# Expert stages: one row tile in four of the closing gated add goes from VectorE to GpSimd

## The reference, cut to what matters

```python
# block 2 (stage l0f): one expert per row
idx = jnp.argmax(logits, axis=-1)
gates = softmax(logits)[idx]
for ei in range(8):
    h = gelu(xf @ W1[ei] + b1[ei]); y = h @ W2[ei] + b2[ei]
    out = out + y * (gf * mask)[:, None]
x = x + out
# block 6 (stage l2f): two experts per row
topv, topi = jax.lax.top_k(logits, 2)
topw = softmax(topv)
out = sum over the two experts of topw * expert(xf)
x = x + out
```

## Time and profile before

| what | us |
|---|---|
| median of 3 runs | 2441.24 |
| the three runs | 2441.24, 2434.01, 2441.58 |
| time of the profiled execution | 2440.11 |
| its span in the profile | 2438.3 |
| VectorE busy in it | 1604.2 (66%) |
| TensorE busy in it | 1987.9 (82%) |
| GpSimd busy in it | 951.7 (39%) |

### The profile page before, as it was taken

How to read it: one execution, slowest core, us unless ns; L and a number is a source line. 1 busy time by engine, 2 the same in 40 slices (tenths; PEclk the granted TensorE clock), 3 DMA queues, 4 the chain that set the end, 5 groups by cost and what they waited for, 6 DMA issues and landing times. The chain is left out here.

```text
span 2438.3 us, 40723 instructions
## 1 busy us (share of the span) xinstructions
PE 1987.9 (82%) x13441; PEld 1621.2 (66%) x13441; DVE 1604.2 (66%) x5274; ACT 1183.1 (49%) x3293; POOL 951.7 (39%) x919
## 2 busy tenths in 40 slices
PE   8985999599948967976999947777878778777888
PEld 5663898499937855655999935566656666665555
DVE  6776111588974237854111168999999999995786
ACT  3544232455421115543333325687777787875444
POOL 3311454300007023303555425666666666662210
PEclk9997999655779989987999965577777678757899
DMA  3112565520315012315354330000000000101442
GB/s 97 62 47 84 205 240 177 150 37 1 108 48 182 0 65 74 101 36 184 130 205 161 106 123 25 1 31 18 31 18 31 31 1 31 49 1 63 164 157 77
DMA packets 101861, 204.50 MB, mean 84 GB/s; under 512 B 20158, under 2 KB 70550, under 8 KB 93718
## 3 DMA queue, kind: packets, MB, share of 16 engines
q1 hardware_dynamic: 77568, 116.19, 14.3%
q0 software_dynamic: 23808, 85.50, 10.2%
q10 hardware_dynamic: 280, 0.23, 0.0%
HBM read 216.24 MB, written 55.28 MB: 111 GB/s over the span
## 5 line engine op out<-in xcount | busy, mean ns | idle before, releaser
L833 DVE MATCH_REPLACE8 l3a_left<-l3a_top,l3a_left 128x256 f32<-128x256 f32 x768 | 308.3, 409 | 0.0
L826 DVE MAX8 l3a_top<-l3a_left 128x8 f32<-128x256 f32 x768 | 285.5, 413 | 0.0
L525 POOL TENSOR_TENSOR l3a_prob<-l3a_expd,l3a_rest 128x512 f32<-128x512 f32 x128 | 162.8, 1272 | 211.4 <-ACT l3a_rest L608 210.4
L363 PEld LDWEIGHTS l3a_psO<-l3a_probT,l3a_vp 128*128 128x128 f32 x1024 | 185.5, 269 | 69.7 <-ACT l3a_probT L624 40.6
L363 PE MATMUL l3a_psO<-l3a_probT,l3a_vp 128*128 128x128 f32 x1024 | 210.0, 370 | 24.7 <-ACT l3a_probT L624 24.6
L345 PE MATMUL l3a_psT<-all_ident,l3a_prob 128*128 128x128 f32 x512 | 112.8, 361 | 106.0 <-POOL l3a_prob L525 105.2
L512 POOL TENSOR_TENSOR l3a_kept<-l3a_raw_sc,l3a_mone 128x512 f32<-128x512 f32 x128 | 163.7, 1279 | 71.9 <-ACT l3a_raw_sc L592 67.9
L2043 ACT ACTIVATE l2f_hT<-l2f_psH,l2f_wt 128x128 f32<-128x128 f32 x312 | 89.2, 369 | 209.8 <-PE l2f_psH L1997 209.8
L518 POOL TENSOR_TENSOR l3a_sc_sb<-l3a_kept,l3a_mlow 128x512 f32<-128x512 f32 x128 | 164.1, 1282 | 10.0
L345 PEld LDWEIGHTS l3a_psT<-all_ident,l3a_prob 128*128 128x128 f32 x512 | 80.0, 186 | 123.9 <-POOL l3a_prob L525 123.4
L2403 PE MATMUL dtw_psS<-dtw_r,all_shift 128*128 128x1 f32 x596 | 152.7, 356 | 10.2 <-DVE dtw_r L2583 9.8
(11 more groups left out here) (599 smaller groups left out, 4730.4 us busy)
## 6 DMA issues: line engine op xcount, KB each, us to landing
key_at<-l3a_a_k SPq DMA_DIRECT2D x8, 768.0 KB, 3.3
kv_at<-dtw_vd SPq DMA_DIRECT2D x8, 512.0 KB, 2.8
k_at<-dtw_kx SPq DMA_DIRECT2D x8, 512.0 KB, 4.2
l1f_kx<-k_at SPq DMA_DIRECT2D x8, 512.0 KB, 4.5
kv_at<-l1f_k SPq DMA_DIRECT2D x8, 512.0 KB, 3.2
l2a_k<-kv_at SPq DMA_DIRECT2D x8, 512.0 KB, 5.6
l2a_vd<-kv_at SPq DMA_DIRECT2D x8, 512.0 KB, 6.6
l2f_yb<-rows_y SPq DMA_DIRECT2D x8, 512.0 KB
```

What stands on the lines that cost most here:

```text
L363: mm = nc.tensor.matmul(psO[y % 2][:, c, 0:P], vp[:, p, kc, c, g * P:g * P + P], probT[:, u % 2, kc, e, :], start=(j == 0 and e == 0 and k ...
L525: nc.gpsimd.tensor_tensor(prob[:, u % 4, :, :], expd[:, u % 2, :, :], rest[:, u % 2, :, :], ALU.subtract).then_inc(picked, 1)
L826: ins = nc.vector.max(top[:, e, eight], rows[:, e, :] if r else scores[:, e, :])
L833: ins = nc.vector.match_replace(out=rows[:, e, :], in_to_replace=top[:, e, eight], in_values=rows[:, e, :] if r else scores[:, e, :], imm_ ...
```

## The change

VectorE now adds three of each group's four row tiles. GpSimd adds the fourth, `t = 4 * g + 3`, after its last scatter. It does it with two instructions in place of one: `tensor_scalar` multiplies the tile of `yb` by the gate in place, `tensor_tensor` adds it to `x`. GpSimd waits for its own multiplication (`weighed`) and, for the second choice, for its own first addition (`added_too`). A semaphore `gated` tells GpSimd that the gates are there; VectorE waits on `gated` where it waited on `step`. In l0f this makes 12 instructions on VectorE and 8 on GpSimd, in l2f 24 and 16.

```diff
-        b_turned, b_read, h_done, g_done, y_ps, y_done, added = (
-            s.sem(n) for n in ("b_turned", "b_read", "h_done", "g_done", "y_ps", "y_done", "added"))
+        b_turned, b_read, h_done, g_done, y_ps, y_done, added, gated, added_too, weighed = (
+            s.sem(n) for n in ("b_turned", "b_read", "h_done", "g_done", "y_ps", "y_done", "added", "gated", "added_too", "weighed"))
...
             scatter(NB - 1)
+            pool.wait_ge(gated, 1)
+            for g in range(NT // 4):
+                pool.wait_ge(back[g], 16 * k_top)
+                t = 4 * g + 3
+                for k in range(k_top):
+                    nc.gpsimd.tensor_scalar(yb[:, k * NT + t, :], yb[:, k * NT + t, :], gate[:, k, t:t + 1], 0.0, ALU.mult, ALU.add)                        .then_inc(weighed, 1)
+                for k in range(k_top):
+                    pool.wait_ge(weighed, k_top * g + k + 1)
+                    if k:
+                        pool.wait_ge(added_too, k_top * g + k)
+                    nc.gpsimd.tensor_tensor(x[:, t, :], yb[:, k * NT + t, :], x[:, t, :], ALU.add).then_inc(added_too, 1)
...
-                then(nc.vector.reciprocal(gate[:, 0, :], gsum[:]))
+                nc.vector.reciprocal(gate[:, 0, :], gsum[:]).then_inc(gated, 1)
+                dve.wait_ge(gated, 1)
...
-                then(nc.vector.tensor_tensor(gate[:, 1, :], gate[:, 0, :], ex[:, :, 0], ALU.mult))
+                nc.vector.tensor_tensor(gate[:, 1, :], gate[:, 0, :], ex[:, :, 0], ALU.mult).then_inc(gated, 1)
+                dve.wait_ge(gated, 1)
...
-                    for t in range(4 * g, 4 * g + 4):
+                    for t in range(4 * g, 4 * g + 3):
                         if k:
-                            dve.wait_ge(added, 4 * k_top * g + t - 4 * g + 1)
+                            dve.wait_ge(added, 3 * k_top * g + t - 4 * g + 1)
```

## The result

The changed kernel takes 2453.07 us (median of 12 runs, 2444.03 to 2461.61) against 2439.51 us (12 runs, 2434.01 to 2441.58). The ratio is 1.0054 with a 95% interval of 1.0038 to 1.0069: slower by 13 us, where 5.6 us were forecast and 2451 was the upper end of the range. The profiled execution took 2453.73 us, with a span of 2451.9.

A forecast was written before the change was run, and what follows sets the result against it. VectorE's adds at the ends of l0f and l2f, 19.2 us of 2440, were taken as the bound; turn-taking with GpSimd adds +1.8 and +3.8 us, so 2440.1 + 5.6 = 2445.7 us, range 2437.5 to 2451.

The forecast's parts named there:

- What bounds the stages: Ends of l0f and l2f: VectorE's adds, 6.42 + 12.75 = 19.2 us, are the bound; nothing else can hide them.
- Edits that cost nothing: Stage ends: swapped semaphore, GpSimd's wait, shared load waits and barrier add nothing; if uncovered, 0.08 us each.
- Alternation: Adding stretches: VectorE's adds and GpSimd's operations block each other and take turns; with +2 to +7.3 us, chance 0.62.
- Rival B: Adding stretches: VectorE's adds always win, GpSimd's chain follows uncovered; +10.6 us, 2450.7; with anything beyond 7.3 us, chance 0.20.
- L897 with its two inputs: VectorE row with two SBUF inputs whose one meeting with GpSimd, ending 1.13 us before L518, stood for the adds.
- The price of alternation: Adding stretches: 8.2 against 6.4 us in l0f, 16.6 against 12.8 in l2f; sum +5.6 us.
- the turn: Time per alternating operation: add after a wait 0.33 us, `tensor_scalar` 0.42, `tensor_tensor` 0.59.
- Rival A: Stage ends: no blocking, engines run side by side; gain 2.4 us, 2437.7; chance 0.14 together with load-paced adds.
- The sign of being wrong at the root: Outside the two stage ends: a stretch changing by more than 1 us would show the forecast wrong.

The follow-up runs named there:

- tail_op: Kernel before plus one tiny GpSimd memset behind VectorE's last add at each expert stage's end: 2451.57 us, ratio 1.0046 to the kernel before.
- early_drain: Changed kernel plus one GpSimd drain right behind its last scatter: 2442.46 us, ratio 1.0018 to the kernel before.
- beside_read: Kernel before, all adds on VectorE, plus 8 (l0f) and 16 (l2f) GpSimd `tensor_tensor` on a tile of its own: 2457.71 us, one execution.
- beside_write: Kernel before, all adds on VectorE, plus GpSimd memsets of 128x256, which read nothing, on its own tile beside them: 2447.84 us, one execution.
- psum_shared: `early_drain` with ScalarE writing VectorE's gate products to PSUM, so its adds read only `x` from SBUF: 2441.06 us, ratio 1.0011 to the kernel before.

## Why the prediction was wrong, point by point

- **What bounds the stages: right.** The adds of 6.42 and 12.75 us and the barrier behind them are the path, and all of the loss but 1.1 us is there.
- **The step that failed** stands under "Edits that cost nothing": "The barrier waits for whichever ends last, as before." It does, but before the change GpSimd's arrival there was 4.2 and 14.9 us early, and I took it for free since its last scatter was issued long ago. Its drain of 7.6 and 4.8 us, hidden in that slack, was in the trace before; I had read the rows of busy engines, where drains don't appear, and never the view of line 54. A GpSimd instruction at the end moved the drain with it. It costs 8.6 of the 12.5 us at the two ends (the gaps grew by 9.0, and 0.4 of that is the last point below); `tail_op` makes it alone, and `early_drain`, which pays it beside the loads, gives 9 us of the median back.
- **Alternation: right.** In the trace of the change each add waits for GpSimd's operation and the other way round, as long as GpSimd has one; two adds run ahead only once, in l2f, while GpSimd waits 0.61 us for a load. Rival B (starving) falls, though the time ended beyond its 2450.7. That L897 with its two inputs stood for the adds was right too. The Trainium skill, page "SBUF — State Buffer", section "Who interferes with whom", says that a VectorE instruction with two SBUF inputs contends with a GpSimd instruction that reads SBUF and not with one that only writes it. The traces agree: 0.69 to 0.94 us for an add in the changed kernel, up to 0.83 in `beside_read`, at most 0.484 in `beside_write`.
- **The price of alternation: two thirds too high.** Forecast +5.6, measured +3.4 (1.2 in l0f, 2.3 in l2f). The term that was mis-sized is the turn. An add behind a wait takes 0.27 to 0.28 us, not 0.33; over the 24 of them that is 1.3 us. And the `tensor_scalar`, priced 0.558 from a form with two scalars per row, takes 0.48 us here when it is alone, so its turn is 0.35, not 0.42; over 12 of them 0.9 us. The turn of the `tensor_tensor`, 0.58 for a forecast 0.59, was right.
- **Rival A: wrong in the loads.** It gave l2f a gain of 1.8 us. `psum_shared` has no exclusion, and the stretch stays at 12.6 us. I had taken the end of the traffic in the earlier trace rows, 1429.2, for the last landing, 8.3 us after the first; in the trace before it is 9.0 us after it, and with GpSimd at work beside the adds 9.6 to 9.7.
- **The sign of being wrong at the root was set too narrow.** It was to be a stretch outside the two ends that changes by more than 1 us. The first stage and the last changed by 1.0, and the first one moves by up to 5.5 us between profiled executions of kernels that don't differ in it.
- **One small thing beside it:** the three new semaphores split the numbers that l2f's end clears into two ranges, and so the barrier runs twice there: the code runs one barrier for each unbroken range of numbers. The view of line 61, before and after:

```profile
L61 POOLq EVENT_SEMAPHORE_RANGE_CLEAR  x1: 175/175/175, 1434.1 to 1434.1; - x1
```

```profile
L61 POOLq EVENT_SEMAPHORE_RANGE_CLEAR  x2: 45/113/181, 1446.5 to 1446.9; - x2
```

The two clears start 0.4 us apart, and that is the second round; it is part of the +2.9.

## What to carry to other kernels

Before an idle engine gets work at the end of a stage, look at its drain there, not only at its last instruction: GpSimd's drain after transfers of its own is long, and it follows whatever comes last. If the work must go there, drain right after the last transfer, while something else is waited for. And where VectorE's instructions have two inputs in SBUF and GpSimd reads SBUF too, price the two by the sum of their turns, and ask whether the loads allow a gain at all, before counting the instructions taken off.

## What the runs showed of the hardware that I had not expected

- GpSimd's drain costs 0.083 us for each transfer that it has issued since the last drain, up to 92 of them, although all had landed (in the changed kernel l0f's were done before the adds began, and it still took 7.6 us). Where more were issued it was shorter: 2.6 us after 118, 4.8 us after 156.
- VectorE's adds with two inputs in SBUF and GpSimd's operations that read SBUF take strict turns (with one SBUF input and one in PSUM, 0.423 to 0.426 us each, they don't), and 128x256 memsets on GpSimd beside the same adds cost them nothing (0.475 to 0.484 us each).
- The changed kernel's runs spread over 17.6 us (2444.03 to 2461.61), the kernel before's over 7.6. GpSimd's drains after l0f and l2f are the same to 0.02 us in all traces that have them undivided, which speaks against them as the cause; but the changed kernel was traced once, and so it stays open.
- In l2f the loads of the results land 9.0 us from first to last, and 9.6 to 9.7 in every trace in which an 8 KB packet of the "instruction" queue falls among them, which happens where GpSimd works beside the adds.
